# Biases of the routed experts: from TensorE to VectorE, ScalarE and GpSimd

## The reference

```python
t = layernorm(x)                                   # 8192 tokens, D = 256
shared = gelu(t @ sw1 + sb1) @ sw2 + sb2
probs = softmax(t @ gate_w + gate_b)               # 8 experts
topk_p, topk_i = top_k(probs, 2)
h = gelu(einsum('td,edf->etf', t, w1) + b1[:, None, :])    # b1: (8, 256)
y = einsum('etf,efd->etd', h, w2) + b2[:, None, :]         # b2: (8, 256)
routed = einsum('te,etd->td', combine, y)          # combine: topk_p at topk_i, else 0
out = x + routed + shared
```

## Time and profile before

| | us |
|---|---|
| median of 3 runs | 2104.12 |
| profiled execution | 2105.01 |
| its span | 2102.2 |
| TensorE busy | 1975.4 (94%) |
| VectorE busy | 1697.7 (81%) |
| ScalarE busy | 1417.6 (67%) |
| GpSimd busy | 1037.6 (49%) |

### The profile page before, as it was taken

The page is one execution under the profiler, slowest core; times in us unless marked ns, Lnnn a source line. Parts: engine busy times, 40 slices in busy tenths (PEclk is TensorE's granted clock), DMA queues, the critical chain, the costliest instruction groups (busy, mean ns, idle before and its releaser), DMA issues.

```text
span 2102.2 us, 35982 instructions
## 1 busy us (share of the span) xinstructions
PE 1975.4 (94%) x12605; PEld 1557.8 (74%) x12605; DVE 1697.7 (81%) x2867; ACT 1417.6 (67%) x2170; POOL 1037.6 (49%) x1204
## 2 busy tenths in 40 slices
PE   6899999999999999999999999999999783999998
PEld 4577777777777777777777777777777562999998
DVE  6678888888888888888888888898988886565565
ACT  6678686868686868686868686868686651444444
POOL 3435454545454545454555555554545453344344
PEclk9999999999999999999999999999999996999999
DMA  4000101010101010101010101010101024764664
GB/s 130 1 21 1 51 1 51 1 51 1 51 1 51 1 51 1 51 1 51 1 51 1 51 1 51 1 51 1 51 1 41 1 71 128 227 190 134 190 183 140
DMA packets 73649, 112.24 MB, mean 53 GB/s; under 512 B 9716, under 2 KB 52219, under 8 KB 73477
## 3 DMA queue, kind: packets, MB, share of 16 engines
q1 hardware_dynamic: 58468, 67.86, 11.4%
q0 software_dynamic: 15008, 42.10, 5.4%
HBM read 63.10 MB, written 48.65 MB: 53 GB/s over the span
## 4 chain that ended last, share of the span: by engine, by line
PE 72%; DVE 15%; ACT 8%; issue 3%; DMA 1%; POOL 0%; SPq 0%; POOLq 0%; DVEq 0%
PE bank_o L1181 10%; PE ring L1161 6%; PE ring L1140 6%; PE ring L1088 5%; PE ring L1166 5%; PE ring L1089 5%; PE ring L1094 5%; DVE norm L766 3%; ACT prob L557 3%; PE bank_d L1192 3%; PE ring L1147 3%; ACT prob L563 2%; PE acc L1201 2%; DVE kT L752 2%; DVE q_lo L757 2%
## 5 line engine op out<-in xcount | busy, mean ns | idle before, releaser
L557 ACT ACTIVATE prob<-ring 128x1024 f32<-128x1024 f32 (+1 forms) x384 | 327.0, 877 | 223.3 <-PE ring L1166 219.6
L766 DVE RECIPROCAL norm<-bank_d 128x512 f32<-128x512 f32 x128 | 429.5, 3356 | 26.8 <-PE bank_d L1192 25.0
L483 POOL TENSOR_SCALAR_AFFINE_SELECT prob<-prob 128x256 f32<-128x256 f32 x512 | 220.0, 450 | 447.5 <-ACT prob L563 447.5
L494 POOL TENSOR_TENSOR key_sum<-prob 128x768 f32<-128x768 f32 x128 | 241.3, 1885 | 345.0 <-PE bank_d L1192 338.2
L563 ACT ACTIVATE prob<-prob 128x1024 f32<-128x1024 f32 (+1 forms) x384 | 344.3, 915 | 5.2
L1181 PE MATMUL bank_o<-prob,v 128*64 128x512 f32 (+3 forms) x2048 | 308.4, 444 | 18.6 <-DVE norm L768 18.6
L752 DVE TENSOR_TENSOR kT<-ring,kT 64x512 fp32r<-64x512 f32 x256 | 176.3, 689 | 124.6 <-ACT kT L570 120.9
L1161 PE MATMUL ring<-qT,kT 128*128 128x256 f32 (+3 forms) x1024 | 239.2, 335 | 32.2 <-DVE xnTl L739 11.8
L1181 PEld LDWEIGHTS bank_o<-prob,v 128*64 128x64 f32 x2048 | 128.2, 138 | 177.3 <-issue 154.9
L1161 PEld LDWEIGHTS ring<-qT,kT 128*128 128x128 f32 x1024 | 165.5, 189 | 110.1 <-issue 50.5
L1166 PE MATMUL ring<-q_lo,kT 128*128 128x256 f32 (+3 forms) x1024 | 225.5, 322 | 0.4 <-DVE q_lo L757 0.4
(11 more groups left out here) (222 smaller groups left out, 4766.6 us busy)
## 6 DMA issues: line engine op xcount, KB each, us to landing
xin<-first SPq DMA_DIRECT2D x71, 257.0 KB, 3.3
xin<-second SPq DMA_DIRECT2D x71, 129.0 KB, 2.7
xin<-base SPq DMA_DIRECT2D x71, 128.0 KB, 2.8
x_next<-in_x SPq DMA_DIRECT2D x16, 512.0 KB, 3.8
x_res<-in_x SPq DMA_DIRECT2D x16, 512.0 KB, 3.8
raw_e<-in_w SPq DMA_DIRECT2D x4, 1024.0 KB, 7.1
first<-pad SPq DMA_DIRECT2D x9, 257.0 KB, 4.8
second<-pad SPq DMA_DIRECT2D x9, 129.0 KB, 5.7
```

Of the source, the lines that this page charges most:

```text
L483: last = nc.gpsimd.affine_select(out=diag, in_=diag, compare_op=ALU.is_ge, fill=0.0, base=0, pattern=[[0, 2], [1, P]], channel_multiplier=-1)
L494: nc.gpsimd.tensor_tensor(key_sum[:, :, :], t0[:, :, P:N], t13[:, :, 0:N - P], ALU.add).then_inc(sum_steps, 1)
L557: nc.scalar.activation(probs[p % 2][u][:, :, :], slot[:, :, 0:UNIT_COLS[u]], ACT.Tanh, scale=SCALE / SOFTCLAMP).then_inc(act_emptied, 1)
L766: nc.vector.reciprocal(norm[:, :], bank_d[:, :]).then_inc(o_steps, 1)
```

## The change

Three things change places.

`b1`: VectorE adds it. A new step `add_bias(n)` reads the product of TensorE from PSUM, adds the expert's row of `b1`, which lies on all 128 partitions, and writes `act_in` in SBUF; the gelu now reads `act_in`.

`b2`: ScalarE multiplies the expert's row of `b2` by the tokens' gate weights (`scale_bias(n)`, into `scaled`, two buffers), and GpSimd adds that to the `BASE` part of `xin` (`add_to_base(n)`) before VectorE weighs the result and adds that part.

TensorE's two matmuls of line 1343 go, and `prepare_bias` with its 16 VectorE operations and four loads. Instead SP loads `b1` and `b2` whole, each spread over 128 partitions (1 MB each), after attention and ahead of `raw_e2`. VectorE and ScalarE now read the experts' numbers from `table` as TensorE does, every 8 tiles.

The diff, cut to its core:

```diff
@@ SP
+            for k, src in enumerate((b1_row, b2_row)):
+                sp.dma_start(b_all[k][:, :], src[0, :].partition_broadcast(P)).then_inc(bias_loaded[k], 16)
             load_experts(1, raw_e2, w2)
@@ GpSimd
-            for k in range(K):
-                nc.gpsimd.memset(b_rows[k][:, :].bitcast(F32), 0.0)
...
+            def add_to_base(n):
+                base_of = xin[n % XIN][:, BASE:]
+                pool.wait_ge(bias_scaled, n + 1)
+                if TILE[n][0] == 1:
+                    loads_before = len([m for m in range(TILES) if m % XIN == n % XIN])
+                    pool.wait_ge(base_loaded[n % XIN], 16 * (n // XIN + 1 - loads_before))
+                nc.gpsimd.tensor_tensor(base_of, base_of, scaled[n % 2][:, :], ALU.add).then_inc(base_biased, 1)
+
             for n, (k, j) in enumerate(TILE):
+                add_to_base(n)
                 pool.wait_ge(y_ready, n + 1)
@@ ScalarE
             def activate(n):
-                act.wait_ge(h_full, n + 1)
+                act.wait_ge(h_biased, n + 1)
...
-                nc.scalar.activation(act_out[n % 2][:, :], ring[0][:, n % 2, 0:FF], ACT.Gelu).then_inc(h_done, 1)
+                nc.scalar.activation(act_out[n % 2][:, :], act_in[n % 2][:, :], ACT.Gelu).then_inc(h_done, 1)
...
+            def scale_bias(n):
+                if TILE[n][1] % BATCH == 0:
+                    weights_of(mybir.EngineType.Activation, n, bias_at)
+                act.wait_ge(xin_loaded[n % XIN], 16 * (n // XIN + 1))
+                if n >= 2:
+                    act.wait_ge(base_biased, n - 1)
+                nc.scalar.activation(scaled[n % 2][:, :], b_all[1][:, bass.ds(bias_at[n], D)], ACT.Copy,
+                                     scale=xin[n % XIN][:, WEIGHT:WEIGHT + 1]).then_inc(bias_scaled, 1)
...
                     in_high(n + 2)
+                scale_bias(n)
                 if n + 1 < count:
                     activate(n + 1)
@@ VectorE
-                    if i == NSEQ - 1 and p in (0, 1, 2, 3):
-                        prepare_bias(p)
...
+            def add_bias(n):
+                if TILE[n][1] % BATCH == 0:
+                    weights_of(mybir.EngineType.DVE, n, bias_at)
+                dve.wait_ge(h_full, n + 1)
+                if n >= 2:
+                    dve.wait_ge(h_done, n - 1)
+                nc.vector.tensor_tensor(act_in[n % 2][:, :], ring[0][:, n % 2, 0:FF],
+                                        b_all[0][:, bass.ds(bias_at[n], D)], ALU.add).then_inc(h_biased, 1)
...
             def weigh(n):
                 dve.wait_ge(y_full, n + 1)
-                if k == 1:
-                    dve.wait_ge(base_loaded[n % XIN], ...)
+                dve.wait_ge(base_biased, n + 1)
...
                     in_low(n + 2)
+                if n + 1 < count:
+                    add_bias(n + 1)
                 act_low(n)
@@ TensorE
-                pe.matmul(dst, ones_r[:, :], biases[:, bass.ds(at, D)], start=False, stop=False)
...
                 if n >= 2:
-                    pe.wait_ge(h_done, n - 1)
+                    pe.wait_ge(h_biased, n - 1)
```

More of the change, by code:

```diff
@@ L109, in block_program @@
 def block_program(nc, x, wqT, wkT, wvT, woT, gate_w, gate_b_rows, w1s, w1, w2s, w2,
-                  b1s_cols, sb2_twice, b1_twice, b2_twice, out):
+                  b1s_cols, sb2_twice, b1_row, b2_row, out):
     first = nc.dram_tensor("first", (ROWS, FIRST_ROW), F32).ap()
@@ L217, in block_program @@
             y_out = [sb(f"y_out{k}", [P, D], F32, arena) for k in range(YOUT)]
+            act_in = [sb(f"act_in{k}", [P, FF], F32, arena) for k in range(2)]
+            b_all = [sb(f"b{k}_all", [P, E * D], F32, arena) for k in (1, 2)]
+            scaled = [sb(f"scaled{k}", [P, D], F32, arena) for k in range(2)]
         head_rows = [slice(0, DH), slice(DH, P)]
-        b_raw = x_next[0:K, :, :].rearrange("p t d -> p (t d)")
         earlier_f = norm[:, 0:P]
@@ L266, in block_program @@
         e_lo = sem("e_lo")
-        bias_loaded = sem("bias_loaded")
+        bias_loaded = [sem(f"bias_loaded{k}") for k in range(2)]
         pad_ready = sem("pad_ready")
@@ L283, in block_program @@
         h_full = sem("h_full")
+        h_biased = sem("h_biased")
+        base_biased = sem("base_biased")
+        bias_scaled = sem("bias_scaled")
         h_done = sem("h_done")
@@ L318, in block_program, with weights_of @@
         TILE = tile_list()
+        def weights_of(engine, n, known):
+            k, j = TILE[n]
+            starts_at = nc.values_load_multi_w_load_instructions(
+                table[K + k:K + k + 1, j:j + BATCH], engines=(engine,), min_val=0, max_val=(E - 1) * D,
+                skip_runtime_bounds_check_because="an expert's number below 8 times 256, or zero")[1]
+            known.update({n + m: at for m, at in enumerate(starts_at) if j + m < TILES})
         BIAS_STEPS = 5
@@ L347, in _ @@
                 sp.dma_start(x_res[:, :, :], x_tiles[i]).then_inc(xres_loaded, 16)
[L349 to L352, removed]
             def load_experts(k, dst, src):
@@ L676, in act_high @@
                                ring[1][:, n % 2, 0:FF].rearrange("p (c t) -> p c t", c=FC)).then_inc(act_hi, 1)
+            bias_at = {}
+            def scale_bias(n):
[6 more added lines that the diff above has]
+                                     scale=xin[n % XIN][:, WEIGHT:WEIGHT + 1]).then_inc(bias_scaled, 1)
             count = len(TILE)
+            act.wait_ge(bias_loaded[1], 16)
+            act.wait_ge(table_ready, 1)
             in_high(0)
@@ L920, in _ @@
             nc.vector.tensor_copy(earlier[:, :], earlier_f).then_inc(bias_steps, 1)
[L922 to L935, removed]
             for i in range(NSEQ):
@@ L1057, in act_low @@
                                         actT[n % 2][0][:, :, :].bitcast(F32), ALU.subtract).then_inc(act_lo, 1)
+            bias_at = {}
+            def add_bias(n):
[6 more added lines that the diff above has]
+                                        b_all[0][:, bass.ds(bias_at[n], D)], ALU.add).then_inc(h_biased, 1)
             def weigh(n):
-                k, j = TILE[n]
                 dve.wait_ge(y_full, n + 1)
-                if k == 1:
-                    dve.wait_ge(base_loaded[n % XIN], 16 * (n // XIN + 1 - len([m for m in range(TILES) if m % XIN == n % XIN])))
+                dve.wait_ge(base_biased, n + 1)
                 if n >= YOUT:
@@ L1070, in _ @@
             count = len(TILE)
+            dve.wait_ge(bias_loaded[0], 16)
             in_low(0)
             in_low(1)
+            add_bias(0)
             for n in range(count):
@@ L1337, in turn_in, with expert_product @@
                 last.then_inc(turned, 1)
-            def expert_product(dst, tokens, weights, biases, at, lo_ready):
+            def expert_product(dst, tokens, weights, at, lo_ready):
                 for c in range(DC):
@@ L1350, in _ @@
             weights_at_tile = {}
[L1352 to L1359, removed]
             def expert_hidden(n):
                 if TILE[n][1] % BATCH == 0:
-                    load_weights_of(n)
+                    weights_of(mybir.EngineType.PE, n, weights_at_tile)
                 pe.wait_ge(in_hi, n + 1)
                 if n >= 2:
-                    pe.wait_ge(h_done, n - 1)
-                expert_product(ring[0][:, n % 2, 0:FF], xinT[n % 2], w_e1, b_rows[0], weights_at_tile[n],
+                    pe.wait_ge(h_biased, n - 1)
+                expert_product(ring[0][:, n % 2, 0:FF], xinT[n % 2], w_e1, weights_at_tile[n],
                                (in_lo, n + 1)).then_inc(h_full, 1)
@@ L1432 @@
         "sb2_twice": twice(L0_ffn_sb2),
-        "b1_twice": twice(L0_ffn_b1),
-        "b2_twice": twice(L0_ffn_b2),
+        "b1_row": laid(np.asarray(L0_ffn_b1).reshape(1, -1)),
+        "b2_row": laid(np.asarray(L0_ffn_b2).reshape(1, -1)),
     }
```

7 lines of the change are left out of this document (1 added, 6 removed).

## The result

The changed kernel takes 2224.39 us (median of 4 runs, 2223.26 to 2225.47) against 2104.74 us (median of 4 runs of the kernel before): ratio 1.0567, 95% interval 1.0553 to 1.0582. It is slower by 120 us.

A forecast was written before the change was run, and what follows sets the result against it. TensorE was taken to set the expert stage's pace; the new GpSimd loop makes it 140 x 3.06 + 10.6 = 439.0 us for 301.9, +137.1. With -17.0 for the last sequence, +120.1 gives 2224 us, range 2190 to 2290.

The forecast's parts named there:

- The GpSimd loop: Expert stage: weighing, send, next add and next weighing form a circle of 3.06 us a tile, against 2.08; chance 0.70.
- latency to the send: Loop term: from the weighing's end to the start of GpSimd's send, 0.80 us, with GpSimd idle.
- hand-over: Loop term: GpSimd's add releasing VectorE's weighing, taken as 0.06 us, bounds 0.03 and 0.25.
- the change of choices: Expert stage, from first to second choices: the step between GpSimd's sends stays at 10.55 us, put as 10.6.
- The add was not contended: Expert stage: GpSimd's add keeps its median of 0.74 us beside VectorE operations with one PSUM input.
- the rival: First: contended add, 1.615 us, 2346 us, chance 0.07. Later: VectorE-ScalarE loop alone, 2.30 us a tile, 2118 us, chance 0.10.
- The last sequence gives 17.0 us: Last sequence: dropping prepare_bias's VectorE work returns 17.0 us in full, bounds 14 and 17.5.
- The loads are covered: Before the expert stage: two 1 MB loads delay raw_e2's landing by some 6 us, at cost 0, cover some 15 us.
- The clock stays: Expert stage: granted clock stays 1.00; the rival, a falling clock, 3.44 us a tile and 2277 us, had chance 0.08.
- TensorE busy for about 60%: Expert stage: expected sign in the changed profile, TensorE's busy share, with the clock at 1.00.
- The second loop: Expert stage: VectorE and ScalarE wait on each other, 2.30 us a tile, hidden under 3.06 with 0.76 us left over.
- the break-even of 2.20: Expert stage: the step in us a tile that decides between a faster and a slower kernel.

The follow-up runs named there:

- e1_ahead: The changed kernel with GpSimd's add of tile n+1 put ahead of its wait for y n, except across the change of choices: 2106.89 us.
- e4_two_adds: The changed kernel with a second GpSimd add of the same size ahead of the one that counts, into an unread buffer: 2307.08 us.
- e9_b2_only: The kernel before with only the second bias moved, to ScalarE and GpSimd in the changed order; first bias and preparation stay: 2241.04 us.
- e7_no_preparation: The kernel before without prepare_bias and its loads; the matmuls of line 1343 stay and add zeros: 2087.98 us against 2105.05 us.
- e8_b1_only: The kernel before with only the first bias moved, to VectorE; the second bias and prepare_bias stay: 2123.97 us, ratio 1.0086.
- e2_ahead_swap: The changed kernel with GpSimd's next add ahead of its wait for y and ScalarE's act_high(n) ahead of activate(n+1): 2058.86 us, ratio 0.9783.

## Why the prediction was right

Forecast 2224 us, measured 2224.4. Step by step:

- **The GpSimd loop sets the step.** Shown by e1_ahead (cut: -117.5 us), e4_two_adds (lengthened by 0.59 us a tile: +82.7 us) and e9_b2_only (alone: +136.0 us). The forecast terms and what the trace has: weighing 0.48 and 0.48, latency to the send 0.80 and 0.80, send 0.97 and 0.99, start of the add behind it 0.01 and 0.02, add 0.74 and 0.66, hand-over 0.06 and 0.09. Sum 3.06 and 3.04. Three terms were 0.01 to 0.03 too low and one 0.08 too high: part of the exactness is luck. The first to last weighing took 439.3 us where 439.0 was forecast, and here too errors cancel: most steps are 3.04 and the change of choices takes 10.14 us where 10.6 was put, and 140 x 3.04 + 10.14 is only 435.7; one step of 5.71 us and two of 3.2 to 3.4 fill most of the difference. The step of 5.71 us holds a send that comes 3.47 us after its weighing ("issue", no other engine). In the kernel before the same send is as late (3.48 us), and there no weighing waits for it; on the loop it costs 2.7 us, which the forecast did not have.
- **The add was not contended.** 628 to 662 ns over 142, below the shortest of line 500. But this kernel does not test contention: VectorE stands idle for the 0.73 us before each weighing, and that is while the add runs. The loop itself keeps the rival away, which the forecast did not say. The test is e1_ahead (second line), where the add at 1880.80 runs beside `y_out` and `in_low`, each with one of its tiles from PSUM:

```profile
L529 POOL TENSOR_TENSOR xin<-xin,scaled x142: 628/655/662, 1775.4 to 2216.7; 128x256 f32<-128x256 f32 x142
L529 POOL TENSOR_TENSOR xin<-xin,scaled x142: 633/656/671, 1775.0 to 2099.3; 128x256 f32<-128x256 f32 x142
```

  The median moves by 1 ns. With this agrees the rule of the Trainium skill, page "SBUF — State Buffer", section "Who interferes with whom", that a VectorE instruction with at most one SBUF input, outside the two-port modes, leaves GpSimd alone.
- **The last sequence gives 17.0 us.** 56.31 us between the reciprocals, and -17.1 us in e7_no_preparation.
- **The loads are covered.** The two of 1 MB are issued at 1721.50, the two loads of `raw_e2` behind them land after 10.7 us instead of 6.5, ScalarE turns to them at 1741.53, and TensorE's first transposes again wait for the token rows, 17.20 us:

```profile
b_all<-in_b_row SPq DMA_DIRECT2D x2, 1024.0 KB, 5.7
raw_e<-in_w SPq DMA_DIRECT2D x2, 1024.0 KB, 10.7
```

- **The clock stays.** 1.00 (2.4 GHz) in the steady stretches. It is lower around the longest waits: 0.88 from 1960 to 2000 us (the change of choices), 0.96 from 2120 to 2160 (the step of 5.71 us), and at the ends of the stage. The forecast was right on a weak row: from 1760 to 1765 us TensorE had a dense run of matmuls until 1762.3 and then nothing, so the row was no case of a stream with short gaps; from 1765 to 1770 us, with TensorE busy for 0.37 us, the clock stood at 0.53. The forecast "TensorE busy for about 60%" is not what the page shows: 32.5 of 40 us, 81%. The count of matmuls is at 61% (208 to 213 for 346). A record is some 0.28 us long where the next matmul starts 0.12 us later, so in a stream with gaps the busy share stays above the share of the work.
- **The second loop was mis-sized.** Put at 2.30 us, it is 2.22 (e1_ahead, e8_b1_only). Its terms in e1_ahead from start to start: `act_low` to `weigh` 0.34, to `in_low` 0.39, to `add_bias` 0.33, to `activate` 0.45, to `act_high` 0.32, to `act_low` 0.39. Five were set 0.01 to 0.04 too high, one (`activate` to `act_high`) 0.04 too low. For the forecast that was without effect; for the rival it was not: it would have given 140 x 2.22 + 10.6 = 321.4, +2.5 us and not +13.7, which is e1_ahead's 2106.9. The case lay so near the break-even of 2.20 that its sign was open, which the text did not say.
- `scale_bias` takes 0.51 us and not 0.39, off the loop.

## What to carry to other kernels

Moving work off the busiest engine is worth its time only if the receivers' order does not close a loop over tiles that is longer than the present step; sum each new circle of waits from start to start and compare it with the present step before counting busy time. Here both biases cost 120 us where they were put, and with two exchanges in the order (the add of the next tile ahead of the wait for this tile's result, the high part ahead of the next gelu) the same placement gains 45 us, 17 of them from the preparation that is gone. Where two loops overlap, the cure of the shorter one measures nothing until the longer one is cut, so a null result of one exchange says little about it.

## What the runs showed of the hardware

In the steady tiles GpSimd's indirect DMA starts 0.80 us after the end of the operation whose result it waits for (0.79 to 0.82 in 139 of the changed kernel's 142 tiles and in 133 of the kernel before), even if GpSimd has been idle. With another GpSimd operation in that time (e1_ahead) nothing is added, so the 0.80 us can be filled; no order tried here shortened it. Where the add ended too late for that, the send started 0.17 us behind it (e2_ahead_swap). A send with an operation queued behind it took 0.99 us instead of 0.97. Ten reads of 16 table values into VectorE's and ScalarE's registers cost more than 36 reads of 4 (2066.1 against 2057.7 us).
